# Attention and sparse FFN: the last two chunks' scores with keys down the partitions

## The reference

```python
xn = _layernorm(x)                                   # (1, 2048, 512)
h = _layernorm(xn) * gamma + beta
q, k, v = h @ qkv[:, :512], h @ qkv[:, 512:1024], h @ qkv[:, 1024:]
scores = where(causal, q @ k.T / sqrt(512), -inf)
attn = softmax(scores) @ v @ o_proj + xn
g = silu(xn @ w_gate) * (xn @ w_up)                  # (1, 2048, 2048)
ffn = keep_2_largest_of_each_4(g) @ w_down
return x + attn + ffn
```

## Time and profile before

| | us |
|---|---|
| three runs | 803.07, 803.34, 803.58 |
| median | 803.34 |
| profiled execution, its own time | 803.29 |
| its span | 801.2 |
| TensorE busy | 796.9 |
| VectorE busy | 578.5 |
| ScalarE busy | 304.2 |

### The profile page before, as it was taken

One profiled execution on the slowest core, in us unless ns is written; L12 is line 12 of the kernel. 1 busy time (PEld: TensorE's weight loads), 2 busy tenths in 40 slices (PEclk: granted clock), 3 DMA queues, 4 the chain that ended last, 5 costly groups with the idle time before them and its releaser, 6 DMA issues.

```text
span 801.2 us, 9529 instructions
## 1 busy us (share of the span) xinstructions
PE 796.9 (99%) x3636; PEld 661.8 (83%) x3636; DVE 578.5 (72%) x998; ACT 304.2 (38%) x498; POOL 10.3 (1%) x21
## 2 busy tenths in 40 slices
PE   9999999999999999999999999999999999999998
PEld 6888888888888888888888888888888888888886
DVE  6978767556633447879989889799558558559786
ACT  5433222123211225564636435364334334335431
POOL 1010101000000000000000000000000000000000
PEclk9999999999999999999999999999999999999999
DMA  9441442040101027566426434497467262261002
GB/s 325 174 159 57 139 135 78 28 144 27 66 27 59 22 95 299 183 251 262 184 76 264 185 80 208 174 361 278 159 217 264 96 237 91 93 237 53 1 0 106
DMA packets 30444, 118.09 MB, mean 147 GB/s; under 512 B 2944, under 2 KB 3008, under 8 KB 27968
## 3 DMA queue, kind: packets, MB, share of 16 engines
q1 hardware_dynamic: 26224, 109.88, 37.0%
q10 hardware_dynamic: 4176, 7.60, 2.8%
HBM read 75.50 MB, written 41.98 MB: 147 GB/s over the span
## 4 chain that ended last, share of the span: by engine, by line
PE 99%; DVE 0%; issue 0%
PE bank L717 13%; PE bank L716 13%; PE bank L715 13%; PE bank L535 10%; PE bank L533 10%; PE bank L534 10%; PE bank L614 8%; PE bank L789 7%; PE bank L791 7%; PE bank L790 7%; PE bank L593 2%; PE bank L661 1%; DVE acc L1291 0%; PE bank L678 0%; PE bank L583 0%; DVE warm L1134 0%
## 5 line engine op out<-in xcount | busy, mean ns | idle before, releaser
L715 PE MATMUL bank<-X_hi,wset 128*128 128x512 f32 x448 | 174.4, 389 | 0.0
L717 PE MATMUL bank<-X_hi,wset 128*128 128x512 f32 x448 | 174.4, 389 | 0.0
L716 PE MATMUL bank<-X_lo,wset 128*128 128x512 f32 x448 | 174.4, 389 | 0.0
L716 PEld LDWEIGHTS bank<-X_lo,wset 128*128 128x128 f32 x448 | 84.1, 188 | 17.5
L715 PEld LDWEIGHTS bank<-X_hi,wset 128*128 128x128 f32 x448 | 84.1, 188 | 17.5
L717 PEld LDWEIGHTS bank<-X_hi,wset 128*128 128x128 f32 x448 | 84.1, 188 | 17.4
L789 PE MATMUL bank<-dw,hs_hi 128*128 128x512 f32 x224 | 87.2, 389 | 0.0
L791 PE MATMUL bank<-dw,hs_lo 128*128 128x512 f32 x224 | 87.2, 389 | 0.0
L790 PE MATMUL bank<-dw,hs_hi 128*128 128x512 f32 x224 | 87.2, 389 | 0.0
L1291 DVE TENSOR_TENSOR acc<-bank,acc 128x512 f32<-128x512 f32 x60 | 40.8, 686 | 41.0 <-PE bank L791 40.5
L533 PE MATMUL bank<-xT_hi,zg_hi 128*128 128x512 f32 (+3 forms) x160 | 58.4, 365 | 0.0
(11 more groups left out here) (171 smaller groups left out, 1363.0 us busy)
## 6 DMA issues: line engine op xcount, KB each, us to landing
w_operands<-wset SPq DMA_DIRECT2D x8, 3584.0 KB, 12.7
wset<-w_operands SPq DMA_DIRECT2D x8, 3584.0 KB, 11.9
wsum<-w_units SPq DMA_DIRECT2D x28, 256.0 KB, 3.5
dw_raw<-L_ffn_w_down SPq DMA_DIRECT2D x14, 512.0 KB, 4.9
xw<-L_attn_x SPq DMA_DIRECT2D x4, 1024.0 KB, 9.6
xt_raw<-x_t SPq DMA_DIRECT2D x8, 512.0 KB, 7.3
xn_t<-xt_raw SPq DMA_DIRECT2D x8, 512.0 KB, 5.2
acc<-resid SPq DMA_DIRECT2D x2, 2048.0 KB, 10.1
```

Of the source, the lines that this page charges most:

```text
L715: pe.matmul(dst[:], u[:, 0, :], x_hi, start=(first and kt == 0), stop=False, skip_group_check=True)
L716: pe.matmul(dst[:], u[:, 0, :], x_lo, start=False, stop=False, skip_group_check=True)
L717: last = pe.matmul(dst[:], u[:, 1, :], x_hi, start=False, stop=(kt == 1), skip_group_check=True)
```

## The change

**Chunks 2 and 3 (token tiles 8 to 15).** Scores are made with 128 keys down the partitions and up to 512 tokens across: one `wide` unit per key tile, 12 for chunk 2 and 16 for chunk 3, the last four of each (the chunk's own) only as wide as causality leaves (512, 384, 256, 128). ACT copies each unit to SBUF. The softmax needs a maximum per token, now down the partitions: DVE keeps a running maximum over two units at a time, folds it (`max_fold`), PE turns it (`max_turn`, 4 transposes), DVE reduces and widens it, PE turns it back over all partitions (`max_spread`, 4), and ACT copies it (`max_keep`). Then the units go in parts (one, one, then pairs): `shift` (DVE subtracts the maximum), `exp_wide` (ACT), `split` (ACT the high part; DVE adds the part to a running sum and makes the low part) and `meet` (PE multiplies it as it is by v, into banks 4 to 7, one per token tile). Row sums are turned once a chunk (`sum_turn`, 4 transposes). Chunks 0 and 1 stay as they were, but `head` now turns all groups of a tile.

**T sums.** `block_sum`, at token tile 5, makes T1 to T4 of the first half in place of the normed input in SBUF and stores them; the FFN then loads them instead of making them. `w_sum` of set 1 and the splits of the X operands become steps of the list.

**SP.** `rows_store` from tile 8 on and `rows_load` from tile 10 on move from ACT's queue to SP's. `load_set(1)` waits until attention is through; `store_set(0)` stands behind it and behind the row stores.

**The last token tile.** The last 128x512 bank of the down product is made as two halves of 256 columns in two banks, added and stored one after the other. POOL makes one more mask.

The core of the diff:

```diff
-                   *stat[3][2:4], x_stats[3], x_rstd[3], xt_load[3], v[2][0]],
-               11: [*z_round[3], *xn[3], xn_store[3], *z[3], v[3][0]]}
+                   *stat[3][2:4], x_stats[3], x_rstd[3], xt_load[3]]}
...
-              5: [v[1][3], xh_pre[2][0], xh[2][0]],
-              6: [xh_pre[2][1], xh[2][1], xh_pre[2][2], xh[2][2]],
-              7: [x_scale[3], xn[2][0]],
-              8: [v[2][1], row_turn[3], row_copy[3], row_store[3], row_spread[3]],
-              9: [v[2][2]],
-              10: [v[2][3], *xh[3][0:2]],
-              11: [v[3][1]],
-              12: [*v[3][2:4], ("w_load", 0, 0)],
-              13: [("w_sum", 0, 0)],
-              14: fills("w_lo", 0)[0:2]}
...
+              5: [v[1][3], xh_pre[2][0], ("block_sum", 0, 0)],
+              6: [xh_pre[2][1], xh[2][0], xh_pre[2][2], xh[2][1], xh[2][2]],
+              7: [x_scale[3]]}
...
+        if i + 1 < OLD:
+            steps += [("scores", i + 1, 0), exp[i + 1]]
+        steps += [*beside.get(i, []), ("attend", i, 0), ("rows", i, 0), ("rows_load", i + 1, 0)]
...
+    def wide_parts(c):
+        own = TC * c
+        return [(0,), (1,), *((u, u + 1) for u in range(2, own + TC, 2))]
...
+    def softmax(c, behind):
+        last = len(wide_parts(c)) - 1
+        order = [shift[c][0], exp_wide[c][0], shift[c][1]]
+        for j in range(last + 1):
+            order += [split[c][j], *exp_wide[c][j + 1:j + 2], *shift[c][j + 2:j + 3], *behind.get(j, []), meet[c][j]]
+        return order
+    u, n = unit[2], 0
+    steps += [*u[0:2], ("rows_store", OLD - 1, 0), row_turn[3], row_copy[3], row_store[3], row_spread[3], *u[2:4], xn[2][0], ("rows_load", OLD + 1, 0),
+              *u[4:6], xn[2][1], xn_store[2], u[6], xh_pre[3][0], u[7], xh_pre[3][1], xh[3][0], u[8], xh_pre[3][2], xh[3][1], u[9],
+              xh_pre[3][3], xh[3][2], *u[10:], xh[3][3], ("max_fold", 2, 0), z_round[3][0], ("max_turn", 2, 0), *z_round[3][1:4], ("max_spread", 2, 0),
+              *z[3][0:2], ("max_keep", 2, 0), *z[3][2:4]]
+    steps += [step for k in range(KT) for step in v[2][k:k + 1]]
+    steps += softmax(2, {2: [xn[3][0]], 4: [xn[3][1], xn_store[3]]})
+    rows_of = {c: [[("rows", n, 0), ("rows_store", n, 0)] for n in range(TC * c, TC * (c + 1))] for c in WIDE}
+    steps += [("sum_turn", 2, 0), *rows_of[2][0], ("rows_load", OLD + 2, 0), *rows_of[2][1], ("rows_load", OLD + 3, 0)]
+    u = unit[3]
+    steps += [*u[0:4], *rows_of[2][2], ("rows_load", OLD + 4, 0), *rows_of[2][3], ("rows_load", OLD + 5, 0), *u[4:], ("max_fold", 3, 0),
+              ("X_load", 0, 0), v[3][0], ("max_turn", 3, 0), v[3][1], ("max_spread", 3, 0), ("max_keep", 3, 0), *v[3][2:4],
+              ("rows_load", NT - 2, 0), ("rows_load", NT - 1, 0), ("w_load", 0, 0)]
+    X_hi_steps, X_lo_steps = ([(kind, i, 0) for i in range(NOP)] for kind in ("X_hi", "X_lo"))
+    w_hi_steps, w_lo_steps = fills("w_hi", 0), fills("w_lo", 0)
+    steps += softmax(3, {2: [("w_sum", 0, 0), *w_hi_steps[0:1]], 3: [*w_hi_steps[1:4], *w_lo_steps[0:2], X_hi_steps[0]],
+                         4: [*w_lo_steps[2:4], X_lo_steps[0]], 5: [X_hi_steps[1], X_hi_steps[2], X_lo_steps[1]],
+                         6: [X_hi_steps[3], X_lo_steps[2]], 7: [X_lo_steps[3]], 8: []})
+    steps += [("T4_load", 0, 0), ("sum_turn", 3, 0), *rows_of[3][0], *rows_of[3][1], *X_hi_steps[4:], *X_lo_steps[4:], *rows_of[3][2], *rows_of[3][3], ("w_sum", 1, 0)]
...
+                elif kind == "block_sum":
+                    for i in range(4):
+                        sp.wait_ge(block_summed, i + 1)
+                        sp.dma_start(t_dram[i], blocks_of(0)[i][:]).then_inc(blocks_stored, 16)
...
+                elif kind == "X_load":
+                    sp.wait_ge(wide_full, N_UNITS)
+                    for c in (0, 1):
+                        sp.wait_ge(xn_stored[c], 32)
+                    sp.wait_ge(blocks_stored, 64)
+                    load_X(X_raw[B11], X_loaded[B11], 0, 0)
+                    load_X(X_raw[B21], X_loaded[B21], 2, 0)
+                    load_T(T2)
+                    load_T(T3)
                 elif kind == "w_load":
-                    sp.wait_ge(prod_full, prod_no["z", NCH - 1, KT - 1] + 1)
-                    sp.wait_ge(prod_full, prod_no["v", NCH - 1, KT - 1] + 1)
+                    sp.wait_ge(prod_full, len(prod_no))
                     load_set(0)
-            sp.wait_ge(prod_full, len(prod_no))
-            for c in (0, 1):
-                sp.wait_ge(xn_stored[c], 32)
-            load_set(1)
+                    load_T(T1)
+                elif kind == "T4_load":
+                    sp.wait_ge(shifted, N_PARTS)
+                    load_X(X_raw[B22], X_loaded[B22], 2, 1)
+                    sp.wait_ge(met, WHOLE_MET)
+                    load_T(T4)
+                    sp.wait_ge(tile_met, len(WIDE) * TC)
+                    load_set(1)
             store_set(0)
-            sp.wait_ge(rows_ready, NT)
-            sp.dma_start(resid_dram[NT - 1], rows[:, (NT - 1) % 2, :]).then_inc(resid_stored, 16)
-            sp.wait_ge(group_attended, len(group_no))
             sp.wait_ge(resid_stored, 16 * NT)
...
+            def meet_values(c, j):
+                pe.wait_ge(wide_ready, parts_ahead[c] + j + 1)
...
+                    for b in range(skip // P, TC):
+                        x = b * P - skip
+                        last = three(bank[4 + b][:], [((hi[:, x:x + P], lo[:, x:x + P]), (v_hi[t // TC][:, t % TC, :], v_lo[t // TC][:, t % TC, :]))],
+                                     first=(u == 0), last=(u == TC * c + b))
+                        if u == TC * c + b:
+                            last = last.then_inc(tile_met, 1)
+                if j < len(wide_parts(c)) - 1:
+                    last.then_inc(met, 1)
...
+                if n == WIDE[-1] and q == 0:
+                    pe.wait_ge(wide_kept, units_ahead[n])
...
+                    if n == WIDE[-1]:
+                        pe.wait_ge(wide_kept, N_UNITS - PROD_RING + 1 + k)
...
+                elif kind == "meet":
+                    u = wide_parts(n)[k][-1]
+                    if u >= TC * n:
+                        pe.wait_ge(prod_free, prod_no["v", n, u - TC * n] + 1)
...
+                    for t in (2, 3):
+                        bank_free(ND - 1, t)
+                    for r in range(G):
+                        down_part(ND - 1, 2, r)
+                        last_part(last_halves[0], r, 0)
+                    pe.wait_ge(added, added_no(ND - 2, 0))
+                    for r in range(G):
+                        last_part(last_halves[1], r, W // 2)
...
                     if n == 2 and k == 0:
-                        act.wait_ge(xn_stored[1], 32)
+                        act.wait_ge(blocks_stored, 64)
...
+                elif kind == "wide":
+                    act.wait_ge(wide_full, units_ahead[n] + k + 1)
+                    nc.scalar.copy(raw_unit(n, k), prod_bank[k % PROD_RING][:, 0:W - unit_cols(n, k)]).then_inc(wide_kept, 1)
+                elif kind == "max_keep":
+                    act.wait_ge(max_spread, n - WIDE[0] + 1)
+                    if n == WIDE[0]:
+                        act.wait_ge(prod_full, prod_no["z", NCH - 1, KT - 1] + 1)
+                    nc.scalar.copy(max_all[n][:], bank[5][:]).then_inc(max_kept, 1)
+                elif kind == "exp_wide":
+                    act.wait_ge(shifted, parts_ahead[n] + k + 1)
+                    nc.scalar.activation(raw_part(n, k), raw_part(n, k), ACT.Exp, scale=SCALE).then_inc(exp_made, 1)
+                elif kind == "split":
+                    act.wait_ge(exp_made, parts_ahead[n] + k + 1)
+                    if k >= 3:
+                        act.wait_ge(met, met_ahead[n] + k - 1)
+                    nc.scalar.copy(hi_part(n, k), raw_part(n, k)).then_inc(wide_hi_ready, 1)
+                elif kind == "X_hi":
+                    X_halves(0, X_ORDER[n:n + 1])
...
+            def shift_part(c, j):
+                if j == 0:
+                    dve.wait_ge(max_kept, c - WIDE[0] + 1)
+                units = wide_parts(c)[j]
+                if units[0] < TC * c:
+                    n = len(units)
+                    block = raw_part(c, j).rearrange("p (u w) -> p u w", w=W)
+                    nc.vector.tensor_tensor(block, block, max_all[c][:].rearrange("p (o w) -> p o w", o=1).broadcast_to((P, n, W)),
+                                            ALU.subtract).then_inc(shifted, 1)
+                    return
...
+                elif kind == "max_fold":
+                    dve.wait_ge(vec_step, wide_done[n])
+                    nc.vector.tensor_tensor(max_one[n][:], max_pair[n][:, 0, :], max_pair[n][:, 1, :], ALU.max).then_inc(max_folded, 1)
+                elif kind == "max_turn":
+                    dve.wait_ge(max_turned, n - WIDE[0] + 1)
+                    done = step(nc.vector.reduce_max(wide_max[:], bank[4][:].rearrange("p (b k) -> p b k", k=P), AX.X))
+                    dve.wait_ge(vec_step, done)
```

(14 more changed lines are left out.)

## The result

The changed kernel takes 818.2 us (median of 6 runs, 817.3 to 819.0) against 803.2 for the kernel before beside it: the ratio is 1.0188, 95% interval 1.0177 to 1.0199. Its profiled execution took 818.8 us, 15.5 more than that of before; the span, from the first to the last instruction, grew from 801.2 to 816.6, by 15.4.

What follows compares the result with a forecast made beforehand. TensorE bounds the kernel: its column count plus any hole cut into it. -7.5 - 0.4 + 9.0 + 2.6 + 3.5 + 3.2 + 4.2 = +14.6 us on 803.3 gave 818 us, range 811 to 822 (806 to 826 with two rivals).

Steps and rivals of the forecast that it cites:

- Hole 1: From v's last product to the first probabilities, chunks 2 and 3: TensorE waits 4.5 us, twice, +9.0.
- Hole 2: Chunk 2's maximum: TensorE waits at max_turn for VectorE's queue of work, +2.6 us (0 to 4).
- Hole 4: Gate and up, n = 0: w_sum(1) behind the rows on VectorE delays the snapshot P5 needs, +3.2 us.
- the tail: Last token tile in halves: shorter addition and store behind the last matmul, -0.4 us (0 to -0.8).
- block_sum at nothing: block_sum's subtractions and stores at token tile 5 were priced at nothing, up to 2 us if cover is short.
- the 36 transposes of probabilities and 24 new ones: Sign to look for in the profile: 36 transposes of probabilities beside 24 new ones, at 0.11 us.
- Hole 5: Late store of operand set 0 delays load_set(2), so P3 of n = 1 waits: +4.2 us (0 to 8).
- Rival B: TensorE's clock falls to half after idle holes: 1.8 us per restart, three make 5.4, 823 us; chance 0.19.
- holes 3 and 5: Hole 3: VectorE falls behind TensorE over the softmax parts of chunks 2 and 3, +3.5 us (0 to 6).
- transposes: TensorE's work: 100 transposes removed at 0.11 us with changes of kind, 11.2 us; 24 added, 2.7 us.
- A: Rival: VectorE and ScalarE run ahead and the DMA drains sooner, Hole 2 and holes 3 and 5 close: 807.6; chance 0.18.
- C: Rival: v products and z rounds hide the whole softmax, giving 795.4 us; chance 0.04.

Runs made afterwards that it cites:

- experiment 3: The changed kernel with w_sum(1) moved ahead of the last two rows steps: 823.5 us, ratio 1.0249.
- Experiment 5: The changed kernel with sixteen unread 512-column matmuls where TensorE waits for the first part of chunks 2 and 3: 819.3 us, ratio 1.0202.
- experiment 1: The changed kernel with shifts, exponentials and splits of the first two parts placed between v's products: 810.1 us, ratio 1.0087.
- experiment 2: The changed kernel with only the first two shifts and first exponential ahead of the last v product, splits staying behind: 814.2 us, ratio 1.0136.

## Why the prediction was right in its number and wrong in its sum

**Right:** the bound (TensorE's columns plus holes), Hole 1 with its whole chain (4.2 against 4.5), Hole 2 (2.3 against 2.6), Hole 4 (3.6 against 3.2; experiment 3 confirms that the place behind the rows makes most of it), the tail, block_sum at nothing (TensorE has no wait near it), the 36 transposes of probabilities and 24 new ones. The landing behind Hole 5 came as forecast too: sums(2) start 33.6 us after gate and up does, against +34.

**Wrong, and first: the clock.** Rival B was given 0.19 and belonged in the sum. Its mechanism came true at each of the three holes; its price of 1.8 per restart, taken from nine matmuls in the earlier trace rows, was too low: 7.8 / 3 = 2.6 us, as 13 or so matmuls start 0.43 apart. Experiment 5 shows the cause, since the spacing goes back to 0.23 when TensorE is kept busy. The Trainium skill (TensorE: Matmul & The Clock Gate, Why this matters for your kernels) warns of half the clock after an idle gap between bursts; the traces agree, with a granted clock of 0.50 behind holes of 2.7 to 9.4 us, though not behind every one: experiment 1 has a hole of 3.6 us without a fall.

**Wrong, second: holes 3 and 5 were added to holes 1 and 4 as if independent.** I sized each with TensorE at full rate behind the hole. In truth TensorE ran at half the clock there while VectorE and the DMA queue went on at their own pace, so what they were behind by was made up inside the slow stretches: 0.6 instead of 3.5, 0.3 instead of 4.2. The sizes themselves were fair: with the clock kept up at the meetings they are 3.6 and 3.0 (experiment 5). That slow stretches and later holes stand in for each other is a mechanism of this kernel. That the two errors, 7.8 too little and 6.8 too much, were nearly equal is luck: nothing in the prediction ties the one to the other. A forecast with rival B added in full would have said 823, too high for this reason.

**Mis-sized:** transposes. I took 0.11 us from eight in a row, plus 0.02 per change of kind, 8.5 for 76 of them. Over all starts of both traces 76 fewer save 7.2 us, 0.095 each; so 1.3 of the gain was not there. Smaller slips, without effect on the argument: 100 at 0.11 and 20 changes at 0.02 are 11.4, not 11.2; +34 less +29.6 is 4.4, not 4.2; and the scores of tokens 8 to 15 are 336 matmuls in both kernels, not 672, a count that the sum doesn't use. The Trainium skill (TensorE: Matmul & The Clock Gate, Part 4: PE-mode transpose) gives about 275 ns. The length of a record agrees, the cost in a stream does not. A group of the changed kernel (count, busy us, mean ns):

```profile
L720 PE MATMUL bank<-ident,raw 128*128 128x128 f32 x36 | 5.2, 272 | 0.0
```

The 36 records last 272 ns each but cover 5.2 us, since they overlap; by its starts a transpose costs a third of the length of its record.

**Rivals.** A (only the hard chains) was wrong in its premise that the other holes close by themselves: they close only while something else holds TensorE up. C (the v products hide the softmax) was false for this order; with the steps in another order the same work runs in 799.4, still 4 us above C's 795.4.

**Still open.** Of experiment 3's P3 wait of 9.4 us, 6.2 follow from TensorE's coming earlier (P5 3.5 sooner, and 2.7 of slow matmuls not there), 0.3 were there before, and 3.0 come from sums(2) starting 3.0 later. The store is issued 1.7 later there, but the loads that sums(2) wait for are issued 2.6 earlier (350.90 against 353.52). Why they land later all the same I did not trace.

## What to carry to other kernels

Closing a wait is worth only the distance to the next one that it was hiding. So size each hole against an otherwise undelayed kernel; then, where a later hole is set by an engine or a queue that keeps its own pace, count only what is left of it after the delays ahead of it, slow stretches included. Here a hole of 2.7 us or more on TensorE cost its length and, in all cases but one, 1.4 to 2.8 us more of slow matmuls, which no view of waits shows: compare matmuls per window and the granted clock. When attention or any stage becomes shorter, look at once which large store or load now falls into the next stage's loads.

## What the runs showed of the hardware that I had not expected

A wait does not always lower the clock. In experiment 1 TensorE waits 3.6 us at P5, the same as in the changed kernel, yet the windows around it and behind it have the full clock, while the 2.9 us wait at P3 of n = 1 is followed by a fall (windows of experiment 1):

```profile
332.00:338.00 6.00, 4.26 (x19) 3.53 (x20) 3.34 (x4) 5.37 (x9) 0.00 (x0) 1.00 1.21 459
338.00:344.00 6.00, 6.00 (x28) 4.97 (x27) 5.32 (x8) 1.63 (x3) 0.00 (x0) 1.00 0.72 222
356.00:362.00 6.00, 3.44 (x9) 2.70 (x10) 5.49 (x7) 6.00 (x10) 0.00 (x0) 0.77 0.58 249
```

Nor is the price fixed: the same 3.6 us wait at P5 was followed by 2.7 us of lost time in the changed kernel and 1.6 in experiment 2, and the 4.2 us hole of chunk 2, with the same steps around it, by 2.3 in the changed kernel and 1.6 in experiment 3. What decides between them these runs don't show. That a slow TensorE can hide so much of what VectorE and a DMA queue are behind by, 5.7 us of waits for 4.7 of slow matmuls in experiment 5, was the other surprise.
